# Band and corner products of a chunked RWKV-7 layer: four 64-row positions, two banks of the second ring, and a new sequence of steps

## The chip, the cores and the metric

The kernel runs on one core of a Trainium2 chip. The metric is the device time of one launch in microseconds. A core has TensorE (PE in the profile; its weight loads are PEld), VectorE (DVE), ScalarE (ACT), GpSimd (POOL) and SyncE (SP). Each runs its own list of instructions, and they meet at semaphores. TensorE reads SBUF and writes PSUM, which has eight banks of 128 partitions x 512 f32.

## What is computed

The input `x` is 2 x 4096 x 256. It is normalised; one branch is an RWKV-7 attention layer, the other a gated FFN with weights from integers; the output is `x + s * silu(ffn)`. Cut to what matters here:

```python
xn = layernorm(x)
# attention: r, w, k, v, a, g are small projections of xn mixed with the token before
def step(S, inp):                       # per batch row and head, S is 64 x 64
    rt, dt, kt, vt, at, bt = inp
    sa = einsum('bhij,bhj->bhi', S, at)
    S = S * dt[:, :, None, :] + sa[..., None] * bt[:, :, None, :] + vt[..., None] * kt[:, :, None, :]
    return S, einsum('bhij,bhj->bhi', S, rt)
# groupnorm of y, bonus term, gate, output projection -> s
gate, up = xn @ w_gate.T, xn @ w_up.T   # 256 -> 768
ffn = (silu(gate) * up) @ w_down.T
out = x + s * silu(ffn)
```

## The kernel before, in words

**Tiles and sections.** The 4096 tokens of both batch rows are cut into NT = 16 tiles of 256 tokens, each tile into QC = 8 chunks of 32 tokens. `sections()` runs over i = -1 to 17. In section i four tiles are at work: `norm` of tile i+1, the projections, decays and pair matrices of tile i, `ffn` and `back` of tile i-1, and `output` of tile i-2. So the chunk recurrence of one tile is mixed with the projections of the next and with the FFN, which fills TensorE between the links of the recurrence.

**What sets the order.** Each engine has a string of letters, one letter a step: `ORDER` for sections 1 to 15, `FIRST` for the sections before, `LAST` for those behind. `walk` takes the next step of the stream with that letter (L norm, F mixing, K key, R receptance, V value, E update, X pairs, D decays, N ffn, B back, O output). Steps stand in the generator functions and end with a `yield`. The strings say nothing of times: an engine that comes to a wait stands still.

**The recurrence.** A chunk is solved as a triangular system, so `back` needs the inverse of 32x32 matrices. VectorE inverts the two 16x16 diagonal blocks of 64 matrices (`inv0` to `inv14`, L1192 and L1196, then `flip`). The lower left block of the inverse is a product of three: TensorE multiplies the stored middle block with the first inverse (the **band**, L563), ScalarE copies that back to SBUF (L893), TensorE multiplies it with the second inverse (the **corner**, L571), ScalarE copies it (L897), and SyncE sends it by way of DRAM into `TT`. Eight matrices of 16 rows stand under each other in 128 rows, and half of them (64 rows) are one block diagonal product of 64x64. There are 16 such products for the band and 16 for the corner in a tile: 8 groups g, and row halves r = 0 and 64. Rows r of the operands give partitions r of the result.

**Positions.** A product with 64 rows of weights and 64 columns takes a quarter of the array: its row half is where the operands stand in SBUF, its column half where the result stands in PSUM. Band and corner use (0, 0) and (64, 64). The products of the recurrence (L614 state, L642 s; with 32 rows L589 values, L598 y, L628 u) use all four pairs of halves, 8 products a group, in two banks.

**The rings.** Of the eight banks, four are the first ring (`bank`, helper `room`) and four, in two `chunk` tensors, the second (`spare`, helper `early_room`). A step takes the next bank of its ring and waits until what stood there four takes ago has been emptied. `early_room(t, ...)` also waits for `y_out(t - 2)` and `st_ready(t - 2)`, since from the values of chunk 0 on the second ring's banks belong to the recurrence (`banks_of`). Band and corner each take one bank of the first ring.

**The chain of the chunks.** state (L614) -> ScalarE `rhs` (L904) -> u (L628) -> ScalarE (L910) and VectorE (L1206) copy into `VU` -> s (L642) -> VectorE `ST` (L1211) -> the state of the next chunk. `y{c}` (L598) ends a chunk's output, which ScalarE takes out (L887).

**The mix.** `norm` ends with the products mix0 (L401) and mix1 (L406), one of each for four mixtures n. VectorE makes `VU` from them (L981, eight of 128x512, n by n, mix0 before mix1), GpSimd adds the token itself (L1284, signal `moved`). The lora product (letter F, L380 with 112 rows) waits for `moved(t, 2)`, the first `k` product for `moved(t, 4)`. The transposes of the keys (KT0 to KT3, L517) belong to `pairs`. vT0 and vT1 (L479) are the transposed values, which ScalarE copies in four pieces each (L784).

## Time and profile before

| what | us |
|---|---|
| median of three runs | 1607.89 (1607.43 to 1608.68) |
| the profiled execution | 1604.9 |
| its span | 1603.4 |
| TensorE busy | 1520.5 (95%) |
| VectorE busy | 1243.6 (78%) |
| ScalarE busy | 1069.5 (67%) |
| GpSimd busy | 354.6 (22%) |

The profile is one execution; times below are microseconds from the start of its span. An f32 product is two records of TensorE, so a group of 16 products has 32 records (a transpose is one record). The duration of a group in the timeline runs from its first start to its last end, and the next group starts before that end, since products overlap: the time that a group takes of the engine is from its start to the start of the next. "Idle before" names the engine and the line that ended the idle time. Some records can be missing.

### The profile page before, as it was taken

To read this page: it belongs to the slowest core of one execution; us is meant where nothing else is said; L and a number is where in the kernel's file an instruction comes from. 1 tells how busy PE (TensorE), PEld (TensorE's weight loads), DVE (VectorE), ACT (ScalarE), POOL (GpSimd) and SP (SyncE) were. 2 spreads that over 40 slices of the span, in tenths; PEclk is the share of its full clock that TensorE was granted. 3 is DMA by queue.
4 is the path that set the end of the run, shared out by engine and by line. 5 is a ranking of instruction groups with operands and counts; after the bars stand their busy time and mean duration, and the time that the engine had idled before them with its cause. 6 is when DMAs were issued, how large, how long until landed. Compare 5 with 4: busy or idle time off the path is not lost.

```text
span 1603.4 us, 48245 instructions
## 1 busy us (share of the span) xinstructions
PE 1520.5 (95%) x20288; PEld 1064.9 (66%) x20288; DVE 1243.6 (78%) x2661; ACT 1069.5 (67%) x1889; POOL 354.6 (22%) x362
## 2 busy tenths in 40 slices
PE   3699999999999999999999999999999999999887
PEld 1366767576676757667676676757667675766765
DVE  2968787787878878887887878778787887888643
ACT  3758586685857758685775858668585775768512
POOL 3121402313040131302213140231304013130201
PEclk9799999999999999999999999999999999999999
DMA  4011110301212021111202111030121202111020
GB/s 149 14 25 29 33 34 16 62 18 32 43 25 47 16 55 25 33 34 24 56 16 39 42 34 34 16 62 19 33 42 25 48 16 55 25 33 34 12 56 28
DMA packets 251430, 57.85 MB, mean 36 GB/s; under 512 B 223696, under 2 KB 250704, under 8 KB 251088
## 3 DMA queue, kind: packets, MB, share of 16 engines
q1 hardware_dynamic: 241936, 41.95, 13.9%
q10 hardware_dynamic: 9280, 12.81, 2.2%
q8 instruction: 162, 2.65, 0.7%
q14 instruction: 52, 0.43, 0.1%
HBM read 36.38 MB, written 18.35 MB: 34 GB/s over the span
## 4 chain that ended last, share of the span: by engine, by line
PE 92%; DVE 3%; ACT 2%; issue 1%; POOL 0%; DMA 0%; SPq 0%; ACTq 0%; DVEq 0%; POOLq 0%
PE bank L534 23%; PE chunk L380 15%; PE bank L544 11%; PE bank L509 8%; PE bank L664 4%; PE chunk L642 3%; PE chunk L614 3%; PE chunk L589 3%; PE chunk L598 2%; PE bank L485 2%; PE bank L380 2%; PE bank L517 2%; PE bank L479 2%; PE chunk L628 2%; DVE VU L981 1%
## 5 line engine op out<-in xcount | busy, mean ns | idle before, releaser
L1325 POOL TENSOR_TENSOR SF<-ST,CT 128x256 f32<-128x256 f32 x128 | 99.7, 779 | 728.8 <-DVE ST L1211 728.8
L534 PE MATMUL bank<-xT,wg 128*128 128x256 f32 x768 | 197.2, 391 | 14.2 <-DVE VU L981 13.5
L534 PE MATMUL bank<-xT,wu 128*128 128x256 f32 x768 | 207.3, 395 | 0.0
L544 PE MATMUL bank<-wd,hT 128*128 128x256 f32 x768 | 176.8, 383 | 1.9 <-DVE hT L1171 1.9
L534 PEld LDWEIGHTS bank<-xT,wg 128*128 128x128 f32 x768 | 136.3, 189 | 57.6 <-DVE VU L981 24.1
L544 PEld LDWEIGHTS bank<-wd,hT 128*128 128x128 f32 x768 | 143.3, 190 | 29.3 <-issue 7.2
L534 PEld LDWEIGHTS bank<-xT,wu 128*128 128x128 f32 x768 | 135.1, 188 | 34.8 <-issue 14.5
L380 PE MATMUL chunk<-KS,W 128*128 128x512 f32 x320 | 149.6, 598 | 0.3 <-ACT gT L719 0.3
L509 PE MATMUL bank<-qpad,KS 128*64 128x32 f32 x4096 | 141.2, 226 | 4.0 <-DVE KE L1143 4.0
L887 ACT ACTIVATE Y<-chunk 32x256 f32<-32x256 f32 x256 | 96.3, 376 | 70.9 <-PE chunk L598 67.0
L509 PEld LDWEIGHTS bank<-qpad,KS 128*64 128x64 f32 x4096 | 130.7, 141 | 14.1 <-issue 9.0
L380 PE MATMUL chunk<-big,W 128*112 128x512 f32 (+1 forms) x256 | 117.9, 593 | 5.1 <-POOL big L1284 2.9
L861 ACT ACTIVATE sg<-bank 128x512 f32<-128x512 f32 x96 | 57.1, 595 | 86.4 <-PE bank L534 84.5
L1171 DVE TENSOR_TENSOR hT<-sg,bank 128x512 f32<-128x512 f32 x96 | 65.7, 684 | 53.0 <-ACT sg L861 35.2
L904 ACT ACTIVATE rhs<-chunk 96x256 f32<-96x256 f32 x128 | 48.5, 379 | 87.3 <-PE chunk L614 86.3
L1206 DVE COPY VU<-chunk 32x256 f32<-32x256 f32 x128 | 53.4, 417 | 63.3 <-PE chunk L628 62.1
L380 PEld LDWEIGHTS chunk<-KS,W 128*128 128x128 f32 x320 | 59.2, 189 | 62.9 <-issue 48.5
L830 ACT ACTIVATE qpad<-big 64x256 f32<-64x256 f32 x256 | 92.2, 407 | 1.9
L1284 POOL TENSOR_TENSOR KS<-VU,xT 128x512 f32<-128x512 f32 x64 | 89.0, 1424 | 0.0
L1284 POOL TENSOR_TENSOR big<-VU,xT 128x512 f32<-128x512 f32 x64 | 74.4, 1198 | 48.4 <-DVE VU L981 48.4
L1211 DVE TENSOR_TENSOR ST<-SF,chunk 128x256 f32<-128x256 f32 x128 | 53.8, 420 | 37.2 <-PE chunk L642 34.4
L380 PEld LDWEIGHTS chunk<-big,W 128*112 128x112 f32 (+1 forms) x256 | 46.5, 182 | 49.7 <-issue 39.4
(156 smaller groups left out, 3231.3 us busy)
## 6 DMA issues: line engine op xcount, KB each, us to landing
smalls<-in_x SPq DMA_DIRECT2D x32, 256.0 KB, 3.1
Y<-in_x SPq DMA_DIRECT2D x32, 256.0 KB, 3.0
out<-fsil ACTq DMA_DIRECT2D x32, 256.0 KB, 2.6
scrA<-AM SPq DMA_DIRECT2D x64, 64.0 KB, 1.9
hat<-scrB SPq DMA_DIRECT2D x32, 128.0 KB, 3.1
hat<-scrF SPq DMA_DIRECT2D x32, 128.0 KB, 3.1
KE<-scrA SPq DMA_DIRECT2D x64, 32.0 KB, 2.2
scrT<-KE SPq DMA_DIRECT2D x16, 128.0 KB, 1.7
```

The lines of the kernel that those rows point to most:

```text
L380: m = pe.matmul(o, weights[:, h, :], x[:, h, :], start=(h == 0), stop=(h == NH - 1))
L509: q = pe.matmul(oc[:, :, BL * j:BL * j + BL], K[:, 2 * n + b, 64 * j:64 * j + 64], Q[:, 2 * n + b, j, :, :, :].rearrange("p a b e -> p (a ...
L534: q = pe.matmul(o[:, TT_ * n2:TT_ * n2 + TT_], w[:, h, 128 * (n + n2):128 * (n + n2) + 128], x_now[:, h], start=(h == 0), stop=(h == NH - 1))
L544: q = pe.matmul(o[:, 256 * m:256 * m + 256], hT[:, n, 128 * m:128 * m + 128], wd[:, n, :], start=(n == 0), stop=(n == NF - 1))
L664: q = pe.matmul(o[:, 256 * n2:256 * n2 + 256], yb[:, h, 128 * m:128 * m + 128], wo[:, h, :], start=(h == 0), stop=(h == NH - 1))
L830: i = act.activation(Q[p0:p0 + 64, :, :, hh, x, :], own[p0:p0 + 64, qs], ACT.Copy)
L861: act.activation(sg[:, :], ring.tile(key)[:, :], ACT.Silu).then_inc(*sg_ready.up)
L887: i = act.activation(by_batch, RY[64 * x + 32:64 * x + 64, :, :].rearrange("p b (g n) -> p b g n", g=NH), ACT.Copy)
L1171: i = dve.tensor_tensor(hT[:, n:n + 2, :], sg[:, :].rearrange("p (n c) -> p n c", n=2), ring.tile(key)[:, :].rearrange("p (n c) -> p n c", ...
L1211: dve.tensor_tensor(ST[:, :, :, :].rearrange("p b h n -> p b (h n)"), SF[:, :, :, :].rearrange("p b h n -> p b (h n)"), PS, ALU.add).then_ ...
L1284: pool.tensor_tensor(columns(dst[:, h, :]), columns(w[:, h, :]), x_now_of(par, h), ALU.add).then_inc(*moved.up)
L1325: pool.tensor_tensor(SF[:, :, :, :], ST[:, :, :, :], fade[:, c].unsqueeze(3).to_broadcast([128, B, NH, N]), ALU.mult).then_inc(*faded.up)
```

## The change

- The band takes two banks of the second ring. Groups g = 2 g2 + x: those with x = 0 go to the first bank and stay on positions (0, 0) and (64, 64); those with x = 1 go to the second bank, with their result in the other half (z = r ^ 64), so on (0, 64) and (64, 0). The four products of one g2 are issued one behind the other.
- ScalarE copies the band in two halves (x = 0, 1; 4 x 64 columns each) into `upper`. For x = 1 the two row halves of `upper` now stand swapped.
- The corner reads `upper` and `late` at z and writes at r, so its result stands where it stood before. It too takes two banks of the second ring and two copies.
- `late` must be swapped as `upper` is for x = 1: SyncE loads it with three transfers instead of one.
- Waits that named the first ring's corner bank name both of the second ring's.
- The four strings of `ORDER` are new. `FIRST` and `LAST` stay.

```diff
-ORDER = {"pe": ("NNNFNKOOFNNORVNNNNKKOVKRBNKBNRNNVBBNBBNBNBNBBVNNBBEBVBBNBBVBNBBNBBXBXBBNXBBNBNBBXBBXBXBBNBBLBNBBXXBB"
-            "LXXXXLL"),
+ORDER = {"pe": ("FNNKONNOFNONKKNNNNOVKVNRNBKBRNRNNBBNBBNBNBBVBBVBEBNNBBVBBNBNBBVBBNBXBBXBBNBNBBNXBBXXBXBBNBBLBBXNBBX"
+            "LXXXLLX"),
...
-        late_loaded, corner_ready, corner_stored = signal("late_loaded", 1, 16), signal("corner_ready"), signal("corner_stored", 1, 16)
+        late_loaded, corner_ready, corner_stored = signal("late_loaded", 3, 16), signal("corner_ready"), signal("corner_stored", 1, 16)
...
-                o = room((t, "band"), band_ready(t))
-                for g in range(8):
-                    for r in (0, 64):
-                        q = pe.matmul(o[r:r + 64, 64 * g:64 * g + 64], upper[r:r + 64, g, :], first[r:r + 64, g, :], start=True, stop=True)
-                q.then_inc(*ring.fill((t, "band")))
+                two = [early_room(t + 1, (t, "band", x), band_ready(t)) for x in range(2)]
+                for g2 in range(4):
+                    for x, o in enumerate(two):
+                        for r in (0, 64):
+                            z = r ^ 64 * x
+                            q = pe.matmul(o[z:z + 64, 64 * g2:64 * g2 + 64], upper[r:r + 64, 2 * g2 + x, :], first[r:r + 64, 2 * g2 + x, :], start=True, stop=True)
+                            if (g2, r) == (3, 64):
+                                q.then_inc(*spare.fill((t, "band", x)))
                 yield "band"
-                o = room((t, "corner"), corner_ready(t))
+                two = [early_room(t + 1, (t, "corner", x), corner_ready(t)) for x in range(2)]
                 pe.wait_ge(*late_loaded(t))
                 pe.wait_ge(*band_ready(t))
-                for g in range(8):
-                    for r in (0, 64):
-                        q = pe.matmul(o[r:r + 64, HL * g:HL * g + HL], upper[r:r + 64, g, :], late[r:r + 64, g, :], start=True, stop=True)
-                q.then_inc(*ring.fill((t, "corner")))
+                for g2 in range(4):
+                    for x, o in enumerate(two):
+                        for r in (0, 64):
+                            z = r ^ 64 * x
+                            q = pe.matmul(o[r:r + 64, HL * g2:HL * g2 + HL], upper[z:z + 64, 2 * g2 + x, :], late[z:z + 64, 2 * g2 + x, :], start=True, stop=True)
+                            if (g2, r) == (3, 64):
+                                q.then_inc(*spare.fill((t, "corner", x)))
...
-                act.activation(upper, ring.tile(key)[:, :].rearrange("p (g n) -> p g n", n=64), ACT.Copy).then_inc(*band_ready.up)
+                for x in range(2):
+                    key = (t, "band", x)
+                    act.wait_ge(*spare.full(key))
+                    i = act.activation(upper[:, x::2, :], spare.tile(key)[:, 0:256].rearrange("p (g n) -> p g n", n=64), ACT.Copy)
+                i.then_inc(*band_ready.up)
...
-                sp.dma_start(late, d["scrT"][64:128].rearrange("(g m) t n -> (m t) g n", m=8)).then_inc(*late_loaded.up)
+                rest = d["scrT"][64:128].rearrange("(g m) t n -> (m t) g n", m=8)
+                sp.dma_start(late[:, 0::2, :], rest[:, 0::2, :]).then_inc(*late_loaded.up)
+                for r in (0, 64):
+                    sp.dma_start(late[r:r + 64, 1::2, :], rest[64 - r:128 - r, 1::2, :]).then_inc(*late_loaded.up)
```

**What the new strings move.** First TensorE from the last steps of a section into the next, at the mix products of `norm` (L401, L406); L517 are transposes of keys, L509 a pair matrix, L534 gate (wg) and up (wu), L380 on 112 rows the lora product, on 128 rows k0, L655 (now L661) the transposes of `output`. Before:

```order
L509 MATMUL bank<-qpad,KS 64x4x8 x32
L517 MATMUL bank<-con,KE 128x128 x4
L401 MATMUL chunk<-smalls,W 128x512 x4
L406 MATMUL bank<-smalls,W 128x512 x4
L534 MATMUL bank<-xT,wg 128x256 x4
L534 MATMUL bank<-xT,wu 128x256 x2
L380 MATMUL chunk<-big,W 112x512 x2
L534 MATMUL bank<-xT,wu 128x256 x2
L380 MATMUL chunk<-big,W 128x512 x2
```

And now:

```order
L509 MATMUL bank<-qpad,KS 64x4x8 x32
L401 MATMUL chunk<-smalls,W 128x512 x4
L406 MATMUL bank<-smalls,W 128x512 x4
L517 MATMUL bank<-con,KE 128x128 x4
L380 MATMUL chunk<-big,W 112x512 x2
L534 MATMUL bank<-xT,wg 128x256 x4
L380 MATMUL chunk<-big,W 128x512 x2
L661 MATMUL bank<-con,Y 128x128 x4
L534 MATMUL bank<-xT,wu 128x256 x4
```

The last key transposes (KT3) moved from ahead of the mix to behind it, where they take the bank of the first ring that L406's first product filled, and the lora product moved ahead of the gate and up products.

Next TensorE around band and corner; L446 are the kk and mk products, L454 the norm products `rn` (64 rows, 64 columns), L380 the v, g and r projections. Before:

```order
L446 MATMUL bank<-smalls,W 128x512 x4
L380 MATMUL chunk<-KS,W 128x512 x2
L563 MATMUL bank<-hat 64x64 x16
L534 MATMUL bank<-xT,wu 128x256 x2
L454 MATMUL bank<-KS,con 64x512 x4
L571 MATMUL bank<-KE,hat 64x16 x16
L534 MATMUL bank<-xT,wu 128x256 x2
```

And now:

```order
L446 MATMUL bank<-smalls,W 128x512 x4
L380 MATMUL chunk<-KS,W 128x512 x2
L534 MATMUL bank<-xT,wu 128x256 x2
L380 MATMUL chunk<-KS,W 128x512 x2
L534 MATMUL bank<-xT,wu 128x256 x2
L565 MATMUL chunk<-hat 64x64 x16
L454 MATMUL bank<-KS,con 64x512 x4
L576 MATMUL chunk<-KE,hat 64x16 x16
L380 MATMUL chunk<-KS,W 128x512 x2
```

Between band (L565) and corner (L576) only `rn` is left; the up products stand ahead of the band.

Last TensorE at chunk 1, from its state group on (L614, now L620; y is L598 or L604, u L628 or L634, values L589 or L595, s L642 or L648, vT L479). Before:

```order
L614 MATMUL chunk<-ST,hat 64x64 x8
L534 MATMUL bank<-xT,wu 128x256 x2
L598 MATMUL chunk<-VU,AM 64x64 x8
L628 MATMUL chunk<-rhs,TT 64x64 x8
L479 MATMUL bank<-con,bv 128x128 x4
L534 MATMUL bank<-xT,wg 128x256 x4
L589 MATMUL chunk<-VU,AM 64x64 x8
L642 MATMUL chunk<-VU,KT 64x64 x8
```

And now:

```order
L620 MATMUL chunk<-ST,hat 64x64 x8
L604 MATMUL chunk<-VU,AM 64x64 x8
L479 MATMUL bank<-con,bv 128x128 x4
L634 MATMUL chunk<-rhs,TT 64x64 x8
L595 MATMUL chunk<-VU,AM 64x64 x8
L479 MATMUL bank<-con,bv 128x128 x4
L648 MATMUL chunk<-VU,KT 64x64 x8
```

vT0 now stands between y and u, and vT1 behind the values, in place of vT and gate products between u and s. On ScalarE the same stretch now reads, from the copy of chunk 0's u on (L921; L874 is the FFN's silu, L867 the gate's, L915 `rhs`, L893 the y copies, L790 the copies of vT):

```order
L921 ACTIVATE VU<-chunk 32x2x2x64
L874 ACT_TABLE_LOAD
L874 ACTIVATE fsil<-bank 128x512
L867 ACTIVATE sg<-bank 128x512
L915 ACTIVATE rhs<-chunk 96x256
L893 ACTIVATE Y<-chunk 32x2x2x64 x2
L790 ACTIVATE VU<-bank 32x4x128 x2
L921 ACTIVATE VU<-chunk 32x2x2x64
```

Two copies of vT0 have come between the y copies and the u copy of chunk 1 (the last row).

## Rows read from the trace of the kernel before

**Rows 1.** The page: busy time and instructions; the chain that ended last, by engine.
```profile
PE 1520.5 (95%) x20288; PEld 1064.9 (66%) x20288; DVE 1243.6 (78%) x2661; ACT 1069.5 (67%) x1889; POOL 354.6 (22%) x362
...
PE 92%; DVE 3%; ACT 2%; issue 1%; POOL 0%; DMA 0%; SPq 0%; ACTq 0%; DVEq 0%; POOLq 0%
```

**Rows 2.** Windows: length, busy us by engine (instructions), clock, DMA share, GB/s.
```profile
946.80:1041.90 95.10, 93.71 (x1270) 65.83 (x1268) 77.48 (x167) 66.62 (x118) 22.00 (x23) 1.00 0.17 34
```

**Rows 3.** Timeline of TensorE: start us, us, engine line op, tiles, shape, records, idle before.
```profile
967.47 1.89 PE L534 MATMUL bank<-xT,wu 128*128 128x256 f32 x8
969.20 1.89 PE L534 MATMUL bank<-xT,wg 128*128 128x256 f32 x8
...
980.88 1.15 PE L563 MATMUL bank<-hat 64*64 64x64 f32 x32
981.96 1.13 PE L534 MATMUL bank<-xT,wu 128*128 128x256 f32 x4
983.05 1.09 PE L454 MATMUL bank<-KS,con 64*64 64x512 f32 x8
983.96 1.06 PE L571 MATMUL bank<-KE,hat 64*64 64x16 f32 x32
```

**Rows 4.** Timeline of TensorE at chunk 1 of another tile.
```profile
903.64 0.46 PE L614 MATMUL chunk<-ST,hat 64*64 64x64 f32 x16
904.03 1.13 PE L534 MATMUL bank<-xT,wu 128*128 128x256 f32 x4
905.09 0.28 PE L598 MATMUL chunk<-VU,AM 32*64 32x64 f32 x4
...
905.53 1.16 PE L479 MATMUL bank<-con,bv 128*128 128x128 f32 x8
```

**Rows 5.** Timeline of TensorE around the mix products.
```profile
946.30 0.66 PE L517 MATMUL bank<-con,KE 128*128 128x128 f32 x4
946.88 1.14 PE L401 MATMUL chunk<-smalls,W 32*128 32x512 f32 x8
947.85 1.04 PE L406 MATMUL bank<-smalls,W 32*128 32x512 f32 x8
949.77 2.00 PE L534 MATMUL bank<-xT,wg 128*128 128x256 f32 x8 [0.89 <-DVE VU L981]
...
952.47 1.88 PE L380 MATMUL chunk<-big,W 128*112 128x512 f32 x4
```

**Rows 6.** Timeline of VectorE and of GpSimd at the same place.
```profile
948.14 0.75 DVE L981 SCALAR_TENSOR_TENSOR VU<-chunk,vec,big 128x512 f32<-128x512 f32 x1 [1.00 <-PE chunk L401]
948.97 0.75 DVE L981 SCALAR_TENSOR_TENSOR VU<-bank,vec,big 128x512 f32<-128x512 f32 x1
...
949.03 4.65 POOL L1284 TENSOR_TENSOR big<-VU,xT 128x512 f32<-128x512 f32 x4 [0.48 <-DVE VU L981]
953.64 1.09 POOL L1284 TENSOR_TENSOR KS<-VU,xT 128x512 f32<-128x512 f32 x1
```

**Rows 7.** Timeline of ScalarE, at chunk 1 and at the band copy.
```profile
901.03 0.38 ACT L910 ACTIVATE VU<-chunk 32x256 f32<-32x256 f32 x1
...
902.62 1.28 ACT L868 ACT_TABLE_LOAD   x1
...
904.80 1.19 ACT L784 ACTIVATE VU<-bank 32x512 f32<-32x512 f32 x2
...
906.64 0.77 ACT L887 ACTIVATE Y<-chunk 32x256 f32<-32x256 f32 x2
...
982.91 0.57 ACT L893 ACTIVATE hat<-bank 128x512 f32<-128x512 f32 x1
```

**Rows 8.** Timeline of SyncE's transfers around the corner's operand.
```profile
974.40 0.37 SPq L1386 DMA_DIRECT2D KE<-scrT  x1
976.33 1.26 SPq L1391 DMA_DIRECT2D hat<-scrF  x2
```

**Rows 9.** Windows as in rows 2, where the granted clock fell at the end.
```profile
1516.00:1519.00 3.00, 1.52 (x8) 0.82 (x6) 1.80 (x4) 0.60 (x1) 2.44 (x2) 1.00 0.13 22
1519.00:1522.00 3.00, 0.52 (x3) 0.52 (x4) 1.63 (x1) 0.00 (x0) 1.34 (x2) 0.58 0.53 82
```

## What I expected, on record before the run

> **What bounds the kernel now.** I read the busy shares and the chain of waits first [rows 1]. TensorE is busy 95% of the span, and the chain that ends last runs over it for 92%. So the kernel is one stream of TensorE work, and only two things move its time: how long that stream is, and where it stands still. Next the windows [rows 2]: of a section of 95.1 us, TensorE is busy 93.7. VectorE (77.5) and ScalarE (66.6) have room, but either can be late at one place. The same window taken over three other sections gives the same figures to 0.1 us, so I cost one section and multiply by 15, the sections i = 1 to 15 that follow `ORDER`. The 16th band and corner stand in the `LAST` table, which is unchanged.
>
> Then the TensorE timeline. Groups of small products have a pace of their own. The band's 16 products are 32 records (an f32 product is two records) and last 1.15 us; a state group has 8 products, 16 records, and lasts 0.46 us [rows 3, 4]. The state products stand on all four pairs of row half and column half, the band's on two. If each "step" serves every position in use at once, the band is 16 steps and the state group 4, and a step is (1.15 - 0.46) / 12 = 0.0575 us. The corner fits: 32 records, 1.06 us, though it streams 16 columns, not 64 [rows 3]. The count of steps sets the time, not the columns.
>
> Idle time before the change: the largest is behind the mix products, 0.89 us in this section, ended by VectorE's `VU` [rows 5].
>
> **Part 1, products on four positions.** Band and corner each go from 16 steps to 8, which saves 8 x 0.0575 = 0.46 us each. TensorE is the bound at both places, so it all counts: **-0.92 us** a section. Nothing here is unseen: the u products use the same four positions in nearly the same order, with two banks, and an adjacent y and u group, 32 records, take 905.09 to 905.53, 0.44 us [rows 4].
>
> A rule of the Trainium skill speaks against this part: "TensorEngine Tiling (Array Packing)", Gotcha 1, says: "Different row tiles cannot access same PSUM bank simultaneously". Both kernels break it, since the row halves of one bank's products alternate. By that rule the changed groups would keep their 1.08 us and the saving would be nil. Here the state group of 0.46 us writes each bank from both row halves [rows 4], so the trace disagrees; I keep a small chance for it below.
>
> **Part 2, fewer changes of tile shape.** A run of 8 records of `L534` takes 969.20 - 967.47 = 1.73 us, so 4 take 0.86; between small groups 4 take 905.09 - 904.03 = 1.06 us [rows 3, 4]. A small group takes 0.39 us for its 4 steps (0.23). So going to another shape and back costs 0.20 + 0.16, or 0.18 us a change of shape. Counting shapes down the TensorE order of a section I get 66 changes before and 64 now: -0.36 us. Against this, `y0` and `u1` no longer touch (vT stands between). Touching, the two take 0.44 us rather than 0.39 + 0.23, so that loses 0.18. Together **-0.18 us**.
>
> **Part 3, ScalarE.** Each copy out becomes two. The 128x512 band copy takes 0.57 us; a 256-column copy takes 0.38 [rows 7]; so band copies end 2 x 0.38 = 0.76 us after the products and not 0.57. What hides that is TensorE work between band and corner. Before: `L534` x4 (1.09) and rn (0.91) [rows 3]. Now rn alone. From band start: the records end at 0.46 + 0.23 = 0.69, the copies start at 0.76 (0.07 is the usual hand-over) and end at 1.52; the corner can start some 0.1 later, at 1.64. The stream reaches it at 0.51 + 0.91 = 1.42. A wait of **+0.2 us**, if ScalarE is free. It is: its last work before is the `gh` tanh, which I place 0.4 us ahead of the band's end. Bounds: 0 (the copies overlap) to 0.6 (ScalarE late). Before, the band copy ended at 982.91 + 0.57 = 983.48 and the corner began at 983.96: covered.
>
> **Part 4, the sequence, at the mix.** This is the costly one. Mix products start at 946.88 (call it 0). VectorE writes the first two `VU` at 1.26 to 2.01 and 2.09 to 2.84. GpSimd then adds: four adds in 4.65 us from 2.15 on, so the second ends at 2.15 + 2.33 = 4.48 [rows 6]. The lora product needs two adds (`moved(t, 2)`). Before it stood behind 12 records of gate and up work and started at 952.47, or 5.59 [rows 5], when its adds were long done. Now only KT3 (0.56 us [rows 5]) is between. KT3 takes the bank that the second `VU` frees, so it waits as the gate does now, to 2.89; it ends at 3.45; lora waits to about 4.6. **+1.15 us**, a second wait that the first doesn't hide. VectorE and GpSimd hold the same steps in the same order here, and both start from the mix products, so they don't come earlier. Bounds: 0.85 (the adds at the 1.09 us of the quicker ones) and 1.3. The wait for `z` ahead of the lora's consumers I leave as it is: ScalarE has lora's two copies done at about 12.1, and z comes at 12.4.
>
> **Part 5, the sequence, at chunk 1.** ScalarE's order now puts the first half of the vT copies between y0 and the u1 copy, and `s1` on TensorE waits for that copy. From the u0 copy at 901.03: 0.40, a table load 1.28, two copies of about 0.6, `rhs`, y0's two (0.77), then vT's two, 1.19 [rows 7], not before the vT products end. The u1 copy ends 0.1 to 0.2 us later than TensorE needs it. **+0.1 us**, bounds 0 and 0.4. The other chunks keep at least one group of 1 us in each gap between state, u and s.
>
> **Part 6, what costs nothing.** The corner operand is three transfers, not one. SyncE issues it at 974.40 in 0.37 us and then idles to 976.33 [rows 8]; two more issues (about 0.4 each) fit in. Room for band and corner in the second ring waits for hk, v and gh, all copied out before. The waits for `y_out` and `st_ready` of the tile before were met by lora's. The first ring has two takes fewer, a gain only where it is full.
>
> **Sum.** -0.92 - 0.18 + 0.2 + 1.15 + 0.1 = +0.35 us a section, x 15 = +5.3. In `LAST` TensorE is 0.92 shorter and the two ScalarE copies 0.2 longer: -0.7. Total +4.6 on the profiled execution's 1604.9 us, so 1609.5. The median of the runs shown, 1607.89, is 3.0 above that execution; against it I expect **1612.5 us**.
>
> **Rivals.**
> 1. *The new waits stay small.* Only the lora wait stands, at 1.0 us or less, and ScalarE is in time at the corner and at s1. Then -1.10 + 1.0 = -0.1 a section: 1607.89 - 1.5 - 0.7, about 1606, no change. For it: both ScalarE waits are 0.1 to 0.2 us, within what I can read.
> 2. *No new wait at the lora product* (faster). If GpSimd's adds were through by 3.45, parts 1 and 2 would stand nearly alone: -1.10 x 15 - 0.7 = -17.2, or 1591; with the ScalarE waits kept 1595. For it: the mix wait may shorten if VectorE comes earlier relative to TensorE. Against it: VectorE's first `VU` waits for the mix product itself, not for its own queue.
> 3. *The clock falls* (slower). With two waits around 0.56 us of work, TensorE stands still 2.1 us of some 2.7. Around 1516 to 1519 it was busy 1.52 of 3 us, and in the next window the granted clock was 0.58 [rows 9], that is, it fell to the lower of its two levels, 1.2 GHz. If that happened here, the next few us of lora and gate would take up to twice as long: 1.7 to 3.4 us a section, 1638 to 1664 in all, and 1620 to 1630 if in a third of the sections. Against it: the 0.89 us wait never did it in the steady sections (clock 1.00 [rows 2]).
> 4. *Four positions bring nothing* (the change doesn't do what it says): +0.92 x 15 on my sum, 1626.
>
> **How the numbers follow.** Forecast 0.43, rival 1 0.25, rival 2 0.18, rival 3 0.11, rival 4 0.03. I call within 0.2% (3.2 us, 1604.7 to 1611.1) no change, which is about what a measurement of this kernel can tell. The forecast's own spread, from the bounds of parts 3 to 5, is 1606 to 1621, with a fifth of it below 1611.1; that gives slower 0.34 + 0.11 + 0.03 + a little of rival 1 = 0.50, same 0.09 + 0.21 = 0.30, faster 0.20 (rival 2 and the low edge of rival 1). The range runs from 1596, which takes in rival 2 where it keeps the ScalarE waits only in part, to 1627.
>
> **What would show it.** Band and corner groups of 32 records at about 0.69 and 0.6 us, against 1.15 and 1.06. Behind the mix products, `L517` with an idle time ended by VectorE of about 0.9 us, and behind it `L380` on 112 rows with about 1.1 us ended by GpSimd's `big`; this row, 15 times, is the prediction's main claim. At `L576` a wait for ScalarE of 0.1 to 0.3 us. A section would be 95.3 to 95.6 us from one mix to the next. I am wrong if GpSimd ends no wait of the lora product, if the section is under 94.8 us, or if the clock shows less than 1.00 in a steady section.

## The result and the profile after

| | us |
|---|---|
| before, median of the runs beside it | 1608.55 |
| changed, median of five runs | 1626.49 (1624.69 to 1640.13) |
| ratio | 1.0132 (95% interval 1.011 to 1.0153) |
| forecast on record | 1612.5 (1596 to 1627) |
| changed, the profiled execution and its span | 1640.13, 1638.6 |

The change makes the kernel slower by 17.9 us. The direction was forecast, the size was not: 4.6 us were expected. The time lies just inside the range.

The page of the changed kernel, answering to [rows 1] (busy time; the chain that ended last, by engine):

```profile
PE 1535.3 (94%) x20288; PEld 1063.0 (65%) x20288; DVE 1257.2 (77%) x2661; ACT 1077.0 (66%) x1921; POOL 355.4 (22%) x362
...
PE 87%; ACT 5%; DVE 3%; POOL 2%; issue 2%; DMA 0%; SPq 0%; ACTq 0%; DVEq 0%; POOLq 0%
```

GpSimd, which was in the last chain with 0%, is in it with 2%. The windows of two sections, as in [rows 2]: length, busy time by engine, granted clock, DMA share, GB/s.

```profile
866.55:962.60 96.05, 93.44 (x1273) 65.23 (x1272) 78.78 (x166) 67.14 (x120) 22.11 (x23) 1.00 0.16 34
...
576.80:674.50 97.70, 95.10 (x1272) 65.99 (x1269) 78.10 (x166) 67.14 (x120) 22.17 (x23) 0.98 0.16 34
```

Most sections take 96.0 us, 0.90 more than the 95.1 of before. Three of the 13 steady ones take 97.7, and there the granted clock is 0.98 and not 1.00. The TensorE timeline at the mix of the first of these two, answering to [rows 5], and at its band, answering to [rows 3] (start, us, operation, records, idle before):

```profile
866.55 1.14 PE L401 MATMUL chunk<-smalls,W 32*128 32x512 f32 x8
867.48 1.13 PE L406 MATMUL bank<-smalls,W 32*128 32x512 f32 x8
869.48 0.66 PE L517 MATMUL bank<-con,KE 128*128 128x128 f32 x4 [0.87 <-DVE VU L992]
871.16 1.94 PE L380 MATMUL chunk<-big,W 128*112 128x512 f32 x4 [1.03 <-POOL big L1296]
...
902.25 0.69 PE L565 MATMUL chunk<-hat 64*64 64x64 f32 x32
902.77 1.04 PE L454 MATMUL bank<-KS,con 64*64 64x512 f32 x8
903.78 0.66 PE L576 MATMUL chunk<-KE,hat 64*64 64x16 f32 x32
904.37 1.98 PE L380 MATMUL chunk<-KS,W 128*128 128x512 f32 x4
```

This is the forecast's picture: two waits with KT3 between them, the second ended by GpSimd, and band and corner that take 0.52 and 0.59 us from start to next start, where they took 1.08 and 1.00 [rows 3].

The same place in the section that took 97.7 us, and the windows behind the mix of another such section:

```profile
579.82 0.66 PE L517 MATMUL bank<-con,KE 128*128 128x128 f32 x4 [0.87 <-DVE VU L992]
581.46 2.78 PE L380 MATMUL chunk<-big,W 128*112 128x512 f32 x4 [0.99 <-POOL big L1296]
584.03 2.79 PE L534 MATMUL bank<-xT,wg 128*128 128x256 f32 x8
586.66 1.88 PE L380 MATMUL chunk<-big,W 128*128 128x512 f32 x4
```

```profile
965.00:970.00 5.00, 3.47 (x9) 1.71 (x10) 4.49 (x7) 0.60 (x1) 5.00 (x5) 0.81 0.47 63
970.00:975.00 5.00, 5.00 (x19) 3.47 (x19) 2.98 (x4) 0.64 (x2) 4.99 (x4) 0.85 0.37 66
975.00:980.00 5.00, 4.61 (x29) 2.90 (x28) 4.69 (x13) 4.30 (x7) 0.00 (x0) 1.00 0.36 106
```

The waits are the same ones. Behind them the lora product takes 2.78 us and not 1.94, and the gate 2.79 and not 1.90: TensorE has fallen to the lower of its two levels, and the section is 1.65 us longer. In the kernel before no steady section shows that.

**What the forecast didn't have at all** is a wait at chunk 6. TensorE's `s6`, and ScalarE at the same place:

```profile
949.57 0.46 PE L595 MATMUL chunk<-VU,AM 32*64 32x64 f32 x16
950.27 0.46 PE L648 MATMUL chunk<-VU,KT 64*64 64x64 f32 x16 [0.24 <-ACT VU L921]
```

```profile
946.86 0.76 ACT L893 ACTIVATE Y<-chunk 32x256 f32<-32x256 f32 x2 [0.60 <-PE chunk L604]
947.65 2.07 ACT L686 ACTIVATE smalls<-smalls,nmean,rstd 128x256 f32<-128x256 f32 x4
949.75 0.38 ACT L921 ACTIVATE VU<-chunk 32x256 f32<-32x256 f32 x1
```

The new ScalarE string puts the four normalised rows of the next tile (L686) ahead of the u1 copy (L921) on which s6 waits. Against the start that the same pair has elsewhere, s6 is 0.32 us late, in every section.

**Where the 35 us of the profiled execution are.** Read from one L401 to the next: 14 sections that follow `ORDER` are some 0.9 us longer each (the first of them 1.4, a few less), together 12; three falls of the clock add 5; the start is 5.9 longer (73.8 us from the first mix to the second, before 67.8) and the part behind the last mix 12.2 (192.3, before 180.1). The start and this last part (the tail) ran slow in this execution. At the start the products of the first L401 take 2.09 us against 1.14, with the same instructions in the same order and a granted clock of 1.00 in both profiles; from 40 to 50 us the granted clock is 0.50, where that of before is 1.00 until 60. In the tail the clock was low for some 30 us (a window of 32 us has 0.53). A typical run of the changed kernel (1625, mean clock 0.985) can't have both: with 0.9 for the 15th section, which stands behind the last mix, 1608.5 + 12 + 0.9 + 5 = 1626.4 leaves no room for them.

### The profile page after: what moved, and what is told of

It reads as the page before. It is cut to its first block, busy times and chain, and to the rows that moved or that the text cites. A ratio compares the mean times of both kernels' runs of the same rounds, so it can differ in the third digit from the quotient of the medians.

```text
span 1638.6 us, 48401 instructions
## 1 busy us (share of the span) xinstructions
PE 1535.3 (94%) x20288; PEld 1063.0 (65%) x20288; DVE 1257.2 (77%) x2661; ACT 1077.0 (66%) x1921; POOL 355.4 (22%) x362
## 4 chain that ended last, share of the span: by engine, by line
PE 87%; ACT 5%; DVE 3%; POOL 2%; issue 2%; DMA 0%; SPq 0%; ACTq 0%; DVEq 0%; POOLq 0%
PE bank L534 22%; PE chunk L380 16%; PE bank L544 8%; PE bank L509 7%; PE bank L670 4%; PE chunk L648 3%; PE chunk L620 3%; PE chunk L595 3%; PE chunk L604 2%; POOL big L1296 2%; PE bank L485 2%; PE bank L479 2%; PE bank L380 2%; ACT smalls L686 2%; PE chunk L634 2%
## 5 line engine op out<-in xcount | busy, mean ns | idle before, releaser
L1337 POOL TENSOR_TENSOR SF<-ST,CT 128x256 f32<-128x256 f32 x128 | 96.2, 752 | 649.9 <-DVE ST L1223 649.9
L534 PE MATMUL bank<-xT,wu 128*128 128x256 f32 x768 | 204.6, 395 | 0.0
L534 PE MATMUL bank<-xT,wg 128*128 128x256 f32 x768 | 203.4, 398 | 0.0
L544 PE MATMUL bank<-wd,hT 128*128 128x256 f32 x768 | 180.9, 386 | 1.9 <-DVE hT L1183 1.9
L534 PEld LDWEIGHTS bank<-xT,wg 128*128 128x128 f32 x768 | 142.4, 194 | 41.6 <-issue 18.8
L534 PEld LDWEIGHTS bank<-xT,wu 128*128 128x128 f32 x768 | 137.9, 191 | 41.5 <-issue 22.2
L380 PE MATMUL chunk<-KS,W 128*128 128x512 f32 x320 | 153.5, 602 | 0.0
L380 PE MATMUL chunk<-big,W 128*112 128x512 f32 (+1 forms) x256 | 127.1, 632 | 20.6 <-POOL big L1296 19.0
L509 PE MATMUL bank<-qpad,KS 128*64 128x32 f32 x4096 | 139.2, 225 | 5.9 <-DVE KE L1155 5.0
L509 PEld LDWEIGHTS bank<-qpad,KS 128*64 128x64 f32 x4096 | 128.8, 139 | 15.8 <-issue 9.6
L893 ACT ACTIVATE Y<-chunk 32x256 f32<-32x256 f32 x256 | 96.0, 375 | 65.1 <-PE chunk L604 62.2
L1183 DVE TENSOR_TENSOR hT<-sg,bank 128x512 f32<-128x512 f32 x96 | 65.7, 684 | 57.5 <-ACT sg L867 47.3
L848 ACT ACTIVATE KT<-bank 128x512 f32<-128x512 f32 x64 | 38.2, 597 | 98.7 <-PE bank L517 98.3
L380 PEld LDWEIGHTS chunk<-big,W 128*112 128x112 f32 (+1 forms) x256 | 47.7, 192 | 73.0 <-issue 43.0
L380 PEld LDWEIGHTS chunk<-KS,W 128*128 128x128 f32 x320 | 58.0, 189 | 55.1 <-issue 52.3
L734 ACT ACTIVATE KB<-chunk 128x512 f32<-128x512 f32 x32 | 19.1, 597 | 111.9 <-PE chunk L380 110.6
L867 ACT ACTIVATE sg<-bank 128x512 f32<-128x512 f32 x96 | 57.2, 596 | 53.3 <-PE bank L534 39.8
```

The costliest lines, as they stand in the source:

```text
L380: m = pe.matmul(o, weights[:, h, :], x[:, h, :], start=(h == 0), stop=(h == NH - 1))
L509: q = pe.matmul(oc[:, :, BL * j:BL * j + BL], K[:, 2 * n + b, 64 * j:64 * j + 64], Q[:, 2 * n + b, j, :, :, :].rearrange("p a b e -> p (a ...
L534: q = pe.matmul(o[:, TT_ * n2:TT_ * n2 + TT_], w[:, h, 128 * (n + n2):128 * (n + n2) + 128], x_now[:, h], start=(h == 0), stop=(h == NH - 1))
L544: q = pe.matmul(o[:, 256 * m:256 * m + 256], hT[:, n, 128 * m:128 * m + 128], wd[:, n, :], start=(n == 0), stop=(n == NF - 1))
L867: act.activation(sg[:, :], ring.tile(key)[:, :], ACT.Silu).then_inc(*sg_ready.up)
L893: i = act.activation(by_batch, RY[64 * x + 32:64 * x + 64, :, :].rearrange("p b (g n) -> p b g n", g=NH), ACT.Copy)
```

## Experiments

The strings of `ORDER` are quoted by the piece that changes. Section lengths are read from one L401 to the next, without a fall of the clock where there are such sections. Ratios are against the runs of before on the same chip.

| kernel | median us | ratio, 95% interval | section | falls in steady sections |
|---|---|---|---|---|
| before | 1607 to 1609 | 1 | 95.1 | none |
| changed | 1626.49 | 1.0132 (1.011 to 1.0153) | 96.0 | 3 of 13 |
| changed, again | 1625.12 | 1.0116 (1.0087 to 1.0145) | 96.0 | 3 of 13 |
| e1, products alone | 1633.75 (three runs) | 1.0162 (1.0128 to 1.0196) | not read | not read |
| e2, order alone | 1646.33 | 1.0242 (1.0209 to 1.0275) | 96.85 | 6 of 13 |
| e6, two positions | 1646.21 (two runs) | 1.0242 (1.0202 to 1.0282) | 96.85 | 5 of 13 |
| e3, lora later | 1619.34 | 1.0084 (1.0055 to 1.0114) | 95.7 | none |
| e4, KT3 first | 1638.94 | 1.0193 (1.016 to 1.0225) | 96.57 | 7 of 13 |
| e5 (TensorE's string) | 1668.75 | 1.0401 (1.0349 to 1.0454) | 98.9, all with a fall | 13 |
| e10 (and ScalarE's) | 1665.68 | 1.0366 (1.0339 to 1.0392) | 98.9, all with a fall | 13 |
| e13 (and VectorE's) | 1604.16 | 0.9994 (0.9968 to 1.0019) | 95.07 | none |
| e14 | 1606.84 | 0.9993 (0.9963 to 1.0023) | 94.90 | none |
| e15 | 1608.52 | 1.0005 (0.9983 to 1.0026) | 95.18 | none |
| e17 | 1603.3 | 0.9982 (0.9961 to 1.0002) | 94.75 | none |
| e18 | 1599.02 | 0.9948 (0.9929 to 0.9967) | 94.75 | none |

**The two halves apart: e1 and e2.** e1 is the changed kernel with the strings of before and one letter moved.

```diff
-"pe": ...OVKRBNKBNRNNV
+"pe": ...OVKBNKBRNRNNV
```

> The changed band and corner products with the order of before. One letter had to move: the R of the first r product stands behind the corner and not ahead of the band, since the corner's second bank is the one that r takes. My theory (products pay, sequence costs): band and corner save 0.46 us each, so a section goes from 95.1 to about 94.2 us and the time to 1608 - 15 x 0.92 - 0.7 = 1593.5 us, with no wait of the lora product for GpSimd and no fall of the clock in a steady section. Rival (four positions bring nothing, the time of the change comes from the products): 1606 to 1610 us, sections of 95.1.

It took 1633.8 us (median of three executions). The profile comes from a fourth, which took 1672.6 us at a mean clock of 0.93, so its lengths are left aside; its list of TensorE's waits (us in total, times, longest) says what happened:

```profile
PE chunk L565 <- issue: 17.8, 16, 2.2
PE bank L454 <- ACT KS L751: 15.2, 13, 1.3
```

The moved r product (1.9 us) no longer stands ahead of the band, so the band comes 1.9 us sooner and waits 1.1 for what it needs, and rn (L454) behind it waits for ScalarE as long. The band's wait fits its loads: SyncE issued them (`hat<-scrF`) up to 1121.24 and the band began 2.7 us later, at 1123.91; before, it began 3.3 us behind the issue and without a wait. So e1 isn't "products alone", and says nothing of their worth. The letter had to move for a reason that is read from the code and was not run: with the strings of before as they are, the corner would wait for the bank of the r product, which ScalarE copies out only behind the corner.

e2 is the kernel before with the new strings.

> The products of before with the new order. My theory: the section of the changed kernel, 96.0 us, plus the 0.92 that its products save, is 96.9, plus a fall of the clock in some sections: 1626 + 14 to 15 = about 1640 us. Rival (the products bring nothing): the same as the changed kernel, 1626, sections of 96.0. Both expect the lora product to wait for GpSimd about 1.0 us in each section.

Sections of 96.85 and falls of the clock came as my theory had them, the time 6 us above it (more sections fell). So the order alone costs 96.85 - 95.12 = 1.73 us a section, and the products give back 96.85 - 96.02 = 0.83 of it.

**What makes the products quick: e6.** The changed kernel, with each product on the column half of its row half:

```diff
-q = pe.matmul(o[z:z + 64, 64 * g2:64 * g2 + 64], upper[r:r + 64, ...
+q = pe.matmul(o[r:r + 64, 64 * g2:64 * g2 + 64], upper[r:r + 64, ...
```

The corner (z = r) and the load of its operand follow, and the two banks and the order stay.

> The changed kernel with its two banks and its order of products, but each product writes the column half that answers to its row half, so only two of the four 64x64 positions are in use (the operand's load follows). My theory (a step serves every position in use): band and corner start 1.08 and about 1.0 us before what follows them, as before the change, against 0.52 and 0.59 on four positions; a section of 96.0 + 0.83 = 96.9 and 1638 to 1642 us. Rival (it is the two banks that let products run at once): the groups keep 0.52 and 0.59, 96.0 a section, 1626 us.

TensorE's groups by line (us in all, mean ns of one), of e6 and then of the changed kernel, and e6's window of an undisturbed section:

```profile
L565 PE MATMUL chunk<-hat 64*64 64x64 f32 x512 | 18.4, 221 | 0.0
L576 PE MATMUL chunk<-KE,hat 64*64 64x16 f32 x512 | 17.7, 206 | 0.7 <-ACT hat L900 0.7
```

```profile
L565 PE MATMUL chunk<-hat 64*64 64x64 f32 x512 | 11.1, 224 | 1.2 <-issue 1.2
L576 PE MATMUL chunk<-KE,hat 64*64 64x16 f32 x512 | 10.5, 208 | 0.8 <-ACT hat L900 0.8
```

```profile
874.01:970.84 96.83, 94.16 (x1272) 65.93 (x1268) 78.77 (x166) 67.30 (x120) 22.16 (x23) 1.00 0.16 34
```

16 groups of 32 records are busy 1.15 us each on two positions, 0.69 on four. Two banks without the second pair of positions bring nothing: the section is that of e2. A product alone takes as long in both (221 and 224 ns); it is the overlap that changes. Four positions with one bank were not tried, since two products from different row halves would then write the same half of the same bank with nothing between them. The Trainium skill, "PSUM — Partial Sum Buffer", section "PSUM bank collisions raise a hardware error", reports a collision of two TensorE writes from different row tiles into one bank and one quadrant of 32 partitions, beside a quotation of the coarser rule by bank alone. The finer one fits both kernels, in which the two row halves of a bank write different partitions, better than the rule of Gotcha 1 that the prediction weighed; no run here makes such a collision.

**The two waits at the mix: e3 and e4.**

```diff
 e3
-"pe": FNNKONNOF
+"pe": NNFKONNOF
 e4
-"pe": ...LXXXLLX
+"pe": ...LXXXXLL
```

> The changed kernel with one move in TensorE's string: it begins NNF and not FNN, so two gate halves (8 records, 2.1 us) stand between KT3 and the lora product. GpSimd's second add ends 1.0 us after KT3, so the lora wait should be gone whole: section 96.0 - 1.2 = 94.8. If the falls of the clock in the steady sections come from the two waits that stand close together, they go as well: 1626 - 15 x 1.2 - 5 = about 1603 us. Rival (the clock falls for the mix wait alone, or the time is lost in the tail whatever the order of the section): falls stay in every fourth section, 1608 to 1610 us.

```profile
1058.41 0.66 PE L517 MATMUL bank<-con,KE 128*128 128x128 f32 x4 [0.86 <-DVE VU L992]
1059.72 2.00 PE L534 MATMUL bank<-xT,wg 128*128 128x256 f32 x8 [0.66 <-DVE VU L992]
1061.56 1.88 PE L380 MATMUL chunk<-big,W 128*112 128x512 f32 x4
```

The lora wait is gone and so are the falls in the steady sections, but the section only came to 95.7: KT3 has used the bank that the first pair of `VU` freed, and the gate now waits 0.66 us for the next. The 1.2 us that I expected were 0.3. The tail had the 30 us of low clock again, the time varied from 1615 to 1633.

> The changed kernel with KT3 ahead of the mix products again, lora still at the head: the 0.56 us of KT3 no longer stand between the two waits, so one wait of about 2.4 us takes the place of 0.87 + 1.03, and the lora product starts at the same time, as it waits for the same add. The section stays at 96.0 to 96.1 and the time at 1624 to 1628. If the clock looks at how long TensorE stands still in one piece, it falls in more sections than every fourth (each costs 1.65: up to 1645); if it looks at the work in a stretch, as often as now.

```profile
775.60 1.04 PE L406 MATMUL bank<-smalls,W 32*128 32x512 f32 x8
779.27 1.94 PE L380 MATMUL chunk<-big,W 128*112 128x512 f32 x4 [2.63 <-POOL big L1296]
```

One wait of 2.63 us stands where two stood, and the clock fell in 7 steady sections, not 3. I had the section wrong: it grew from 96.0 to 96.57. The lora product waits for a chain that starts at the mix, so KT3 behind the mix was done inside that wait for nothing; ahead of it, it costs its 0.56 us. With e3, this ties the falls to the waiting behind the mix. What e4 can't say is which property of it counts: it is both longer in all (2.6 against 1.9) and in one piece.

**Taking the mix part out: e5, e10, e13.** The three kernels restore the order of before around the mix on one, two and three engines.

```diff
 e5
-"pe": FNNKONNOF...LXXXLLX
+"pe": NNNFNKOOF...LXXXXLL
 e10, in addition
-"act": KNFFFFFFFKK
+"act": NFKFFFFFFKK
 e13, in addition
-"dve": OBONOB
+"dve": ONBOOB
```

> The changed kernel with both ends of TensorE's string as before the change: it begins NNNFNKOOF (three gate and up halves ahead of the lora product) and ends LXXXXLL (KT3 ahead of the mix products). Everything else of the new sequence stays. e3 showed that a gate half right behind KT3 waits 0.8 us for the third VU, since KT3 has taken the one free bank; with KT3 gone from there the gate waits 0.9 us once and nothing else does. My theory: 96.0 - 1.15 = 94.9 us a section, no fall of the clock in the steady sections, so 1626.5 - 15 x 1.15 - 5 = about 1604 us; from the other side, 1608.5 - 15 x 0.25 - 0.7 = 1604. Rival (the rest of the new sequence costs as much as the mix part): sections of 95.3 or more, 1610 us or more.

> The kernel of e5 with ScalarE's string beginning as before the change too (NFK and not KNF: the copies out of the lora product ahead of that of k0). In e5 these copies stood behind the copy of k0, which TensorE now makes later than lora; that made z wait 2.9 us. My theory: that wait falls back to the 0.4 us it has in both kernels, and what is left of the new sequence costs 0.16 at the corner, 0.11 at s1 and 0.32 at s6: 95.1 - 0.83 + 0.6 = 94.9 a section, 1608 - 4 = about 1604 us, no fall of the clock in a steady section. Rival (another engine's order also counts on lora at the head, VectorE's first): z waits 1 us or more, and the clock falls as in e5, 1620 us or more.

> The kernel of e10 with VectorE's string beginning as before the change too (ONBOO and not OBONO: the product hT of a gate pair ahead of the second y tile). In e5 and e10 z waited 2.8 us for this hT, which stood behind work on yT that TensorE makes later. So now all three engines have the order of before around the mix, and all else of the new sequence stays. My theory: z waits 0.4 us as in both kernels; 0.16 at the corner, 0.11 at s1 and 0.32 at s6 are left: 94.9 a section, about 1604 us, no fall of the clock in a steady section. Rival (the new sequence hangs together as a whole and the next engine's wait comes up): 96 us or more a section, 1620 us.

e5 was the slowest of all, but not for the mix. Its z products, and VectorE at that place in e10:

```profile
1102.36 0.70 PE L420 MATMUL chunk<-smalls,W 32*128 32x512 f32 x2 [2.82 <-DVE hT L1183]
```

```profile
988.79 1.43 DVE L1237 TENSOR_TENSOR Y<-Y,st 128x1024 f32<-128x1024 f32 x1
990.15 1.38 DVE L1197 CAST KE<-ti 128x256 f32<-128x256 bf16 x1
991.89 0.88 DVE L1245 SCALAR_TENSOR_TENSOR hat<-bank,vec,bv 128x256 f32<-128x256 f32 x2 [0.36 <-PE bank L661]
992.80 1.48 DVE L1250 SCALAR_TENSOR_TENSOR hat<-hat,vec,gT 128x512 f32<-128x512 f32 x1
994.20 0.68 DVE L1183 TENSOR_TENSOR hT<-sg,bank 128x512 f32<-128x512 f32 x1
```

z needs a bank of the first ring that `hT` (L1183) frees. In the new VectorE string `hT` stands behind output work (the last of it waits for TensorE's transposes L661): it starts 12.9 us behind the mix in e10, where it started at 8.9 before the change. I took ScalarE for the culprit first (its lora copies stood behind that of k0 in e5); e10 put those right, 988.80 to 989.99, and z waited as long, 2.8 us, and started 2.4 us later than in the kernel before. Only e13 took the wait away. With it went every fall in a steady section; the time is 61 us under that of e10:

```profile
853.15:948.22 95.07, 93.39 (x1269) 65.01 (x1268) 78.14 (x167) 67.31 (x120) 22.14 (x23) 1.00 0.17 34
```

95.07 and not 94.9: the mix part of the new order is worth 96.02 - 95.07 = 0.95 us of the section, and the rest of it still eats what the products give.

**The small waits: e8, e11, e15, e17.** e8 and e11 have one ScalarE letter moved, on e5 and e10; e15 has it and a second, on e13; e17 has only the first, on e13.

```diff
 e8, e11, e17
-"act": ...BBBXXBBLBXLBLX
+"act": ...BBBXXBBBLXLBLX
 e15, in addition
-"act": ...NNBBVBVVBVB
+"act": ...NNBBBVVVBVB
```

> The kernel of e5 with one letter of ScalarE's string moved: the normalised rows of the next tile (four operations, 2.07 us) stand behind the u1 copy of chunk 6 and not ahead of it. My theory: the 0.32 us that s6 waits in each section go and nothing takes their place, so 94.9 - 0.3 = 94.6 a section, 4.7 us less than e5, about 1599 us. Rival: the norm transposes, which come 0.4 us behind s6, then wait for the rows instead: no change against e5, 94.9.

> e10 with the u1 copy of chunk 6 ahead of the normalised rows on ScalarE (as in e8, where the 0.32 us at s6 were gone from the trace and no wait came in its place). My theory: 94.6 a section, 4.7 us less than e10, about 1599 us, faster than both kernels. Rival (z waits as in e5): as for e10.

e8 (1666.61 us) and e11 (1660.3) had the z wait of e5 and its falls of the clock, and 0.32 us less at s6 with nothing in its place: sections with one fall take 98.6 us, where those of e5 and e10 take 98.9.

> The kernel of e13 with two letters moved in ScalarE's string: the u1 copy of chunk 1 ahead of the first pair of vT copies, and that of chunk 6 ahead of the normalised rows. TensorE's string is that of e13. My theory: s1's 0.12 and s6's 0.32 us are gone and nothing comes in their place: 95.07 - 0.43 = 94.64 a section, 6.5 us less than e13 in an execution with the same clock, about 1597.5 us. Rival (what TensorE gains it gives back at the next wait): 95.0 a section, 1603 us.

The rival won: 95.18, slower than e13. Both waits were gone, but with the six vT copies together on ScalarE the g product (L485) waited for them:

```profile
1009.55 1.10 PE L485 MATMUL bank<-smalls,W 128*128 128x512 f32 x2 [0.47 <-ACT VU L790]
```

> The kernel of e13 with only the second of e15's two moves: the u1 copy of chunk 6 ahead of the normalised rows on ScalarE. In e15 the other move (u1 of chunk 1 ahead of the vT copies) took 0.12 us away at s1 and brought 0.36 at the g product and 0.18 ahead of a gate, since the vT copies and what they free came later; so it was that move that ate the gain. My theory: 95.07 - 0.31 = 94.76 a section, 4.7 us less than e13 at the same clock, 1599 to 1600 us. Rival (the chunk 6 move is given back as well): 95.05, 1604 us.

94.75 a section, as my theory had it. The move at chunk 1 had eaten the gain; the wait of 0.12 us at s1 is the cheaper side of that trade.

**Work between band and corner: e9, e12, e14.** On top of e8, e11's strings and e13's in turn:

```diff
-"pe": ...VKVNRNBKBRNRNN
+"pe": ...VKVNRBNKBRNRNN
```

> The kernel of e8 with one half of up moved from ahead of the band to behind it, so that 1.0 us more of work stands between the band and the corner: the corner's wait for ScalarE's two copies (0.16 us a section) goes. The band then starts 1.0 us earlier, some 5.4 us behind its loads' issue. My theory: 94.45 a section, 2.4 us less than e8. Rival: the band is now ahead of its loads or of ScalarE's copies of the banks that it takes, as in e1, and waits as long or longer: e8's time or more.

> e11 with one half of up between band and corner (as in e9, where the corner had no wait and the band had none either). My theory: 94.45 a section, 2.3 us less than e11, about 1597 us. Rival: VectorE's or ScalarE's next wait takes it, same time as e11.

> The kernel of e12 with the same move in VectorE's string: order of before around the mix, u1 of chunk 6 ahead of the normalised rows, one half of up between band and corner. My theory: 94.4 a section, 1608 - 15 x 0.7 - 0.7 = about 1597 us, faster than both kernels. Rival: as for e13.

e9 (1667.0 us, median of three executions) and e12 (1658.2) stood under the z wait. e14 and e17 differ in this move alone. e14 has no wait at the corner, 0.16 us less, and yet a section 0.15 us longer:

```profile
851.81:946.70 94.89, 93.45 (x1276) 65.06 (x1268) 78.11 (x166) 67.41 (x121) 22.15 (x23) 1.00 0.17 35
```

The half of up between two groups of 64x64 products adds two changes of tile shape, so one change costs about (0.15 + 0.16) / 2 = 0.15 us, near the 0.18 of the prediction's part 2. The same move on e8 and on e11 says the same: sections with one fall take 98.77 us in e9 and e12, and 98.61 in e8 and e11. The Trainium skill, "TensorEngine Tiling (Array Packing)", section "Key Properties", says that a change of tiling mode drains TensorE, which agrees.

**The added transfers: e18.** In the last tile, which follows `LAST`, the band of the changed kernel waits, and SyncE has issued its loads late (start, us, of each transfer; `scrT<-KE` is the store that the corner's loads wait for, `hat<-scrF` the band's loads). TensorE and SyncE of the changed kernel:

```profile
1564.65 0.69 PE L565 MATMUL chunk<-hat 64*64 64x64 f32 x32 [1.19 <-issue]
```

```profile
1555.63 0.34 SPq L1393 DMA_DIRECT2D scrT<-KE  x1
...
1558.29 0.37 SPq L1399 DMA_DIRECT2D KE<-scrT  x1
1558.70 1.48 SPq L1401 DMA_DIRECT2D KE<-scrT  x2
1560.91 1.25 SPq L1406 DMA_DIRECT2D hat<-scrF  x2
```

e18 is e17 with the two loads of `first` ahead of the three of `late`:

```diff
+sp.dma_start(first[64 * r:64 * r + 64], band(d["scrF"], r)).then_inc(*f_loaded.up)
 sp.dma_start(late[:, 0::2, :], rest[:, 0::2, :]).then_inc(*late_loaded.up)
 sp.dma_start(late[r:r + 64, 1::2, :], rest[64 - r:128 - r, 1::2, :]).then_inc(*late_loaded.up)
-sp.dma_start(first[64 * r:64 * r + 64], band(d["scrF"], r)).then_inc(*f_loaded.up)
```

> The kernel of e17 with SyncE's order changed: the two loads of the band's operand ahead of the three loads of the corner's. In the last tile the band of e13 waits 0.78 us and that of the changed kernel 1.19 where that of before had no wait; I put that down to the two transfers that the change adds ahead of the band's loads (1.24 us of SyncE). My theory: that wait goes, 0.8 us once in the run, the section stays as in e17: 1 us less in the tail of the profile. Rival (the wait is for the flip on VectorE, or the corner's loads now come late in its place): the same wait at the band or a new one at the corner.

```profile
1537.81 0.69 PE L565 MATMUL chunk<-hat 64*64 64x64 f32 x32
1539.34 0.66 PE L576 MATMUL chunk<-KE,hat 64*64 64x16 f32 x32 [0.84 <-ACT hat L900]
```

```profile
1533.89 1.26 SPq L1402 DMA_DIRECT2D hat<-scrF  x2
```

```profile
852.54:947.29 94.75, 93.28 (x1269) 64.98 (x1268) 78.14 (x167) 67.31 (x120) 22.14 (x23) 1.00 0.17 35
```

The wait at the band is gone and no other came: the corner waits 0.84, as it did in the changed kernel (0.83). e18 is faster than both kernels: 0.9948 of before, interval 0.9929 to 0.9967. Its median is 4.3 us below e17's, more than the 0.8 that the wait explains. Five of e17's twelve runs were above 1607 us at mean clocks of 0.982 or less, and one of e18's. So the wait may also set whether the clock stays low in the tail, but that was not shown: both kinds of run occur in both kernels. Of the 19 profiled executions, seven of the twelve whose band waits in the last tile have the long stretch of low clock, and one of the seven whose band doesn't.

The added transfers are only a part of this wait. From the issue of the store into `scrF` to the band's loads it is 2.52 us in the kernel before, 4.97 in e17 and 4.20 in e18: the swap gives 0.77 back, and most of the delay is SyncE waiting longer for its stores to land. In the changed kernel SyncE even stands still from 1560.18 to 1560.91, behind the added transfers and ahead of the band's loads. And e4 and e6, with the same number of transfers in the same order, have no wait at the band. SyncE of e4 in the last tile:

```profile
1567.15 0.34 SPq L1393 DMA_DIRECT2D scrT<-KE  x1
...
1568.88 0.37 SPq L1399 DMA_DIRECT2D KE<-scrT  x1
...
1571.51 1.25 SPq L1406 DMA_DIRECT2D hat<-scrF  x2
```

Here 1.73 us pass from the store to the first load behind it, as before the change (1.72), against 2.66 in the changed kernel and 3.63 in e17. Why the store takes longer there is open.

**The changed kernel again.**

> The changed kernel as it is, a second profile. In the first, TensorE's clock stayed low for 30.7 us behind the last tile's waits, which the profile of before did not show, and the execution took 1640 us where others took 1625. If that is chance, the steady sections are 96.0 again with a fall in some of them, and the tail may be 12 us shorter; if it belongs to the changed kernel, the tail is 192 us again in every profile.

Sections of 96.0, three falls of 1.7 us, and a tail of 192.4 us with the low clock. Both profiled executions of the changed kernel had that tail, at 1640 and 1635 us, while six of its other seven runs took 1624 to 1627. The start was 68.5 us this time, not 73.8: that part of the first profile was chance. What decides on the tail stays open.

## Why the prediction missed, point by point

- **Part 1, four positions: right.** Forecast 0.92 us a section, measured 0.83 (e2 and e6 against the changed kernel). The count of steps, and positions rather than banks or columns, was the right model (e6).
- **Part 2, fewer shape changes: wrong.** The price of a change was about right (0.15, e14 against e17), and the trace has two changes fewer in a section, as counted, but no gain of 0.18 shows. e2's new waits add up to 1.5 us (0.96 at the mix, 0.32 at s6, 0.11 at s1, 0.13 at the corner) and its section grew by 1.73: 0.2 us more, where 0.18 less was forecast. e13 and e17 also come out 0.2 us above the sum of products and waits. By the starts in the trace, y takes 0.21 us more in a section since y0 and u1 no longer touch (forecast 0.18), and the two vT groups take 0.20 more without s1's wait; so the gain of 0.36 that the count promised is spent, and why vT grew is open.
- **Part 3, ScalarE at the corner: right**, 0.16 for 0.2 (from rn's start to the corner's 1.02 us in e13, where the same form of product, L494, takes 0.86 to the next start).
- **Part 4, the lora product: right as a mechanism and nearly in size**, a wait of 1.03 us for 1.15 in each section, ended by GpSimd; taking the whole mix part out was worth 0.95 (e13).
- **Part 5, chunk 1: right, and incomplete.** s1 waits 0.11 for 0.1. But "the other chunks keep at least one group" looked at TensorE's order alone. At chunk 6 ScalarE's own order had moved, and s6 waits 0.32 us in every section (gone in e17).
- **Part 6, the transfers: right in the sections, wrong in `LAST`.** There the band waits 1.19 us for its loads, which is more than the 0.92 that the products save: with this wait the term of -0.7 is +0.5. The added transfers account for about 0.8 of such a wait in e17 (e18), and the rest is the later landing of SyncE's stores, which the forecast didn't have and which stays unexplained.
- **The clock: the rival that I gave 0.11.** The section sum comes to +0.90 for +0.35, 8 us over 15 sections. Another 5 us are the falls, 1.65 us each, in three sections of 13. Rival 3 named the place, the price (1.7 to 3.4) and "a third of the sections", and 1620 to 1630 for it. I discounted it since a wait of 0.89 us had never done it. But two waits of 0.87 and 1.03 us around 0.56 us of work are another thing, and [rows 9], which I quoted beside it, was the nearer row: there TensorE was busy 1.52 of 3 us, and here it stands still for 1.90 of the 2.55 us from the end of the mix to the lora product. When e3 made the waiting shorter the falls were gone; when e4 (2.63 us) and e10 (0.9, then 2.8) made it longer there were more.

So the forecast's step that failed is the sum of +0.35 us a section, which measured +0.90. The two terms that made it too low are the wait at s6, put at nothing because TensorE had a group in each gap (+0.32), and the shape changes, -0.18 that came out as about +0.2 (+0.37); the products gave 0.09 less than forecast, and the mix and the corner cost 0.20 and 0.04 less. On top of it the sum had nothing for the fall of the clock, which was priced as unlikely and took 5 us. That the time still fell inside the range was luck: the forecast's own bounds gave 1606 to 1621, and what carried it to 1626 is in none of them. Rival 4 (four positions bring nothing) would have given nearly the measured time, 1626, and is false: e6 is 20 us slower than the changed kernel. A time that fits is no evidence for its reason.

## What to carry to other kernels

A new order of steps has to be read on every engine, and once for each chain, since the wait that costs may be on an engine whose string the change seems only to follow; e5, e10 and e13 show that this piece of the order could be undone only on all three engines at once. A wait on TensorE is priced twice: what it lasts, and what the clock takes if it stands still near another wait, for which the nearest row with a fallen clock is the measure, not the row with the longest harmless wait. Before a transfer is split, look at what stands behind it on its queue in the stage with the least slack, and at how long the stores ahead of it take to land there.

## What the hardware did that I had not expected

- The clock fell in some executions of the same pattern and not in others: of 13 sections with the same two waits, three fell, 386 us apart both times in the first profile of the changed kernel, 386 and 290 in the second; in e4, with one wait of 2.63 us, 7; in e10, with waits of 0.9 and 2.8 us some eight us apart, all. Each fall cost 1.65 to 1.7 us.
- The low clock in the tail, some 30 us in one piece, came with TensorE nearly always busy:

```profile
1580.00:1612.00 32.00, 30.29 (x505) 21.79 (x504) 5.30 (x12) 10.12 (x26) 3.10 (x5) 0.53 0.01 2
```

It makes an execution 10 to 15 us longer, nearly as much as the whole change, and the changed kernel and those made from it show it in some runs. For kernels that are near each other the mean clock has to be read beside every time.
